# Local attention: one product for values and denominators, and reciprocal norms spread by one bf16 pass over three parts

## What is computed

```python
def l2norm(t):
    return t / jnp.clip(jnp.linalg.norm(t, axis=-1, keepdims=True), 1e-12)
...
h = shift_token(x)
q, k, v = jnp.split(h @ wqkv, 3, axis=-1)            # 8 heads of 64
q = l2norm(q) * qs
k = l2norm(k) * ksc
q, k = rotary_xpos(q, k)
sim = einsum('bhwid,bhwjd->bhwij', bq, bk)           # windows of 64, each sees itself and the one before
attn = jax.nn.softmax(where(mask, -max, sim), axis=-1)
out = jnp.einsum('bhwij,bhwjd->bhwid', attn, bv)
x = x + o @ wo
```

## Time and profile before

| | before |
|---|---|
| median of 3 runs | 6118.09 us (6118.06 to 6119.7) |
| profiled execution, its own time | 6125.03 us |
| its span, first to last instruction | 6123.2 us |
| PE busy | 5316.8 us (87%) |
| DVE busy | 3563.9 us (58%) |
| ACT busy | 3332.0 us (54%) |
| POOL busy | 2568.9 us (42%) |
| mean granted PE clock | 0.946 of 2.4 GHz |

### The profile page before, as it was taken

How to read it: one execution, slowest core, us unless ns; L and a number is a source line. 1 busy time by engine, 2 the same in 40 slices (tenths; PEclk the granted TensorE clock), 3 DMA queues, 4 the chain that set the end, 5 groups by cost and what they waited for, 6 DMA issues and landing times. The chain is left out here.

```text
span 6123.2 us, 113557 instructions
## 1 busy us (share of the span) xinstructions
PE 5316.8 (87%) x39222; PEld 2810.7 (46%) x39222; DVE 3563.9 (58%) x4189; ACT 3332.0 (54%) x4968; POOL 2568.9 (42%) x1902
## 2 busy tenths in 40 slices
PE   5866888888888998999897999899897999787999
PEld 2322555555544554554343554555343444343443
DVE  4757999999964553554354554554554343554444
ACT  4745888888854553554454554455354333443343
POOL 1333999999943662663133662664231000000000
PEclk8986999999999999999898999999899999888999
DMA  1002111111110110110000110111000210001111
GB/s 43 17 10 83 31 31 32 32 30 31 31 52 24 43 43 10 42 42 19 4 15 25 42 42 14 42 41 28 28 15 20 55 41 14 0 0 28 38 33 28
DMA packets 143957, 182.98 MB, mean 30 GB/s; under 512 B 33584, under 2 KB 86960, under 8 KB 142512
## 3 DMA queue, kind: packets, MB, share of 16 engines
q1 hardware_dynamic: 143792, 180.85, 11.1%
HBM read 80.31 MB, written 12.85 MB: 15 GB/s over the span
## 5 line engine op out<-in xcount | busy, mean ns | idle before, releaser
L2502 POOL TENSOR_TENSOR arena<-arena,wbig 128x1024 f32<-128x1024 f32 x512 | 1191.4, 2472 | 107.7 <-ACT arena L2438 107.6
L2489 DVE TENSOR_TENSOR_SCAN arena<-banks,arena 128x1024 f32<-128x1024 f32 x512 | 1140.6, 2278 | 68.4 <-ACT banks L2433 49.4
L963 ACT ACTIVATE arena<-banks,wbig 128x512 f32<-128x512 f32 x512 | 351.8, 687 | 591.2 <-PE banks L921 582.5
L1020 DVE TENSOR_TENSOR arena<-arena 128x512 f32<-128x512 f32 x512 | 353.2, 692 | 470.7 <-ACT arena L963 436.4
L2433 ACT ACTIVATE banks<-banks 128x1020 f32<-128x1020 f32 x512 | 518.1, 1012 | 108.5 <-PE banks L2354 100.9
L1510 POOL TENSOR_TENSOR arena<-arena 128x512 f32<-128x512 f32 x256 | 354.9, 1386 | 527.3 <-DMA arena<-arena 527.3
L635 DVE TENSOR_REDUCE arena<-banks 128x4 f32<-128x1024 f32 (+1 forms) x384 | 401.7, 1046 | 280.0 <-PE banks L462 225.7
L2438 ACT COPY arena<-banks 128x1024 f32<-128x1024 f32 x512 | 520.8, 1017 | 51.2 <-POOL arena L2502 29.9
L571 ACT ACTIVATE Y<-banks 128x2048 f32<-128x2048 f32 x192 | 305.6, 1592 | 306.4 <-PE banks L498 236.4
L931 PE MATMUL banks<-arena,wbig 128*128 128x512 f32 x1024 | 463.5, 598 | 0.0
L921 PE MATMUL banks<-Z,wbig 128*128 x1024 | 459.1, 593 | 0.0
(11 more groups left out here) (304 smaller groups left out, 9887.0 us busy)
## 6 DMA issues: line engine op xcount, KB each, us to landing
arena<-arena SPq DMA_DIRECT2D x1024, 64.0 KB, 2.0
arena<-scratch_g SPq DMA_DIRECT2D x64, 512.0 KB, 10.8
wbig<-wbig SPq DMA_DIRECT2D x48, 240.0 KB, 3.1
wbig<-scratch_d SPq DMA_DIRECT2D x512, 16.0 KB, 1.7
wbig<-scratch_b SPq DMA_DIRECT2D x64, 128.0 KB, 2.2
wbig<-scratch_c SPq DMA_DIRECT2D x64, 128.0 KB, 2.1
arena<-Z SPq DMA_DIRECT2D x64, 128.0 KB, 2.1
wbig<-in_l_ffn SPq DMA_DIRECT2D x1, 4197.0 KB, 12.4
```

The costliest lines, as they stand in the source:

```text
L963: act.activation(hid[e % 2][:, f, :], hbank[f], ACT.Relu, bias=b1[:, e, f:f + 1])\
L1020: last = dve.tensor_tensor(hid[e % 2][:, f, :], hid[e % 2][:, f, :], gate[u][:, e, :], ALU.mult)
L2489: dve.tensor_tensor_scan(own, line(decay_bank[n % 2]), own, 0.0, ALU.mult, ALU.add)\
L2502: pool.tensor_tensor(four(h[par][:, m * 1024:m * 1024 + 1024]), four(us[n % 2]), Bs[par].unsqueeze(1).to_broadcast([128, 4, SEQ]), ALU.mult)\
```

## The change

Three edits in `window_attention_stage`. First, the values tile `v` gets a third slot of ones between the two heads of a group, so that one product with 128 columns of weights gives values in one half of the partitions and denominators in the other; the products with `ones` go away. Head r = 0 has its values in the lower half and its denominators in the upper, head r = 1 the other way round. ACT's logarithm and DVE's multiplication now work on one half of the partitions each, so each becomes two instructions. Second, the reciprocal norm is cut into three bf16 parts: ACT writes it in bf16 (`high`) ahead of the f32 exponential, and DVE makes rest, middle and last part (`norm_parts`), one part to a row within each group of 16. Third, the spreading is a bf16 product over these rows, with a matrix `part_spread` that adds the three parts.

```diff
@@ spread_norms (PE)
                 if n == 0:
-                    pe.wait_ge(act_f.sem, act_f.at(b, "exp"))
+                    pe.wait_ge(dve_p.sem, dve_p.at(b, "parts"))
...
-                    last = pe.matmul(bank[g % 2], k.c64["head_spread"][rows(g), :], rs[rows(g), :],
+                    last = pe.matmul(bank[g % 2], k.cb["part_spread"][rows(g), :], parts[rows(g), :],
@@ values (PE)
                 for c, at, n, first in ((0, 0, 192, 0), (1, 192, 128, 128)):
                     for r in range(2):
-                        pe.matmul(to[half_rows(r), first:first + n], v[par][:, c, 2 * f + r, :],
-                                  prob[f % 2][:, r, at:at + n], start=(c == 0), stop=True, skip_group_check=True)
-                for c, at, n, first in ((0, 0, 192, 0), (1, 192, 128, 128)):
-                    for r in range(2):
-                        last = pe.matmul(to[half_rows(r), SEQ + first:SEQ + first + n], ones[:, 0:WDIM],
-                                         prob[f % 2][:, r, at:at + n], start=False, stop=True, skip_group_check=True)
+                        last = pe.matmul(to[:, r * SEQ + first:r * SEQ + first + n],
+                                         v[par][:, c, f, r:r + 2, :].rearrange("p s d -> p (s d)"),
+                                         prob[f % 2][:, r, at:at + n], start=(c == 0 and r == 0), stop=True,
+                                         skip_group_check=True)
@@ root and reciprocal (ACT)
+                act.activation(high, rs, ACT.Exp, scale=-0.5, bias=k.c64["half_ln"]).then_inc(act_f.sem, 1)
                 act.activation(rs, rs, ACT.Exp, scale=-0.5, bias=k.c64["half_ln"]).then_inc(act_f.sem, 1)
...
-                act.activation(recip[f % 2], obank[f % 2][:, SEQ:2 * SEQ], ACT.Ln).then_inc(act_d.sem, 1)
+                for r in range(2):
+                    last = act.activation(recip[f % 2][half_rows(r), :], obank[f % 2][half_rows(1 - r), r * SEQ:(r + 1) * SEQ],
+                                          ACT.Ln)
+                last.then_inc(act_d.sem, 1)
@@ norm_parts, normalize and trip (DVE)
+            def norm_parts(b):
+                dve.wait_ge(act_f.sem, act_f.at(b, "exp"))
+                dve.scalar_tensor_tensor(out=rs, in0=high, scalar=k.c["rest_minus"], in1=rs, op0=ALU.mult, op1=ALU.add)\
+                    .then_inc(dve_p.sem, 1)
+                dve.wait_ge(dve_p.sem, dve_p.at(b, "rest"))
+                dve.tensor_copy(high, rs).then_inc(dve_p.sem, 1)
+                dve.wait_ge(dve_p.sem, dve_p.at(b, "middle"))
+                dve.wait_ge(pe_f.sem, pe_f.before(b, "norm1"))
+                dve.scalar_tensor_tensor(out=parts, in0=high, scalar=k.c["last_minus"], in1=rs, op0=ALU.mult, op1=ALU.add)\
+                    .then_inc(dve_p.sem, 1)
...
-                dve.tensor_tensor(oT[:, f, :], obank[f % 2][:, 0:SEQ], recip[f % 2], ALU.mult).then_inc(dve_n.sem, 1)
+                for r in range(2):
+                    last = dve.tensor_tensor(oT[half_rows(r), f, :], obank[f % 2][half_rows(r), r * SEQ:(r + 1) * SEQ],
+                                             recip[f % 2][half_rows(r), :], ALU.mult)
+                last.then_inc(dve_n.sem, 1)
...
                 reduce(b, 3)
+                if more:
+                    norm_parts(b + 1)
                 normalize(b, 1)
```

More of the change, by code:

```diff
@@ L1085, in window_attention_stage @@
     pe_w = Steps(k, "mixed", ["wo"], BATCH)
-    act_f = Steps(k, "squares", ["cp0", "sq0", "sq1", "cp2", "sq2", "sq3", "ln", "exp", "hb"], BATCH)
+    act_f = Steps(k, "squares", ["cp0", "sq0", "sq1", "cp2", "sq2", "sq3", "ln", "high", "exp", "hb"], BATCH)
     act_e = Steps(k, "exponentials", ["e0", "v", "e1", "e2", "e3"], BATCH)
@@ L1095, in window_attention_stage @@
     pool_f = Steps(k, "sides", [f"{s}{f}" for f in groups for s in ("sin", "add")] + [f"low{f}" for f in groups], BATCH)
+    dve_p = Steps(k, "norm_parts", ["rest", "middle", "parts"], BATCH)
     pool_h = Steps(k, "shifted", ["low", "high"], BATCH)
@@ L1109, in window_attention_stage @@
     rs = take(TILE)
+    high, parts = k.arena.take_bf16(TILE), k.arena.take_bf16(TILE)
     cos_w, sin_w = take(TILE), take(TILE)
@@ L1112, in window_attention_stage @@
     qkb = pairs(k.arena.take_bf16(8 * SEQ), 8)
-    v = [take(2 * 512).rearrange("p (c h d) -> p c h d", c=2, h=WHEADS) for _ in range(2)]
+    v = [take(2 * 4 * 192).rearrange("p (c f s d) -> p c f s d", c=2, f=4, s=3) for _ in range(2)]
     prob = [pairs(take(2 * 320), 2) for _ in range(2)]
@@ L1122, in window_attention_stage @@
     obank = [k.psum[:, 6 + n, :] for n in range(2)]
-    cleared = Count(k, "cleared", 5)
+    cleared = Count(k, "cleared", 7)
     ones = k.c["ones"]
@@ L1135, in _ @@
             dve.memset(mx, 0.0).then_inc(cleared.sem, 1)
+            for par in range(2):
+                dve.memset(v[par][:, :, :, 1, :], 1.0).then_inc(cleared.sem, 1)
             for m, (scale, partner) in enumerate(((w["qs"], w["qp"]), (w["ks"], w["kp"]))):
@@ L1141, in _ @@
                     .then_inc(cleared.sem, 1)
-            dve.wait_ge(cleared.sem, cleared.at(5))
+            dve.wait_ge(cleared.sem, cleared.at(7))
     with nc.Block() as block:
@@ L1348, in values_in @@
                 for c in range(2):
-                    last = act.copy(v[par][:, c, :, :].rearrange("p h d -> p (h d)"), bank[c])
+                    last = act.copy(v[par][:, c, :, 0:3:2, :], bank[c].rearrange("p (f r d) -> p f r d", f=4, r=2))
                 last.then_inc(act_e.sem, 1)
@@ L1411, in _ @@
         def _(dve):
-            for s in (dve_f, dve_r, dve_n, dve_y):
+            for s in (dve_f, dve_r, dve_n, dve_y, dve_p):
                 s.prime(dve)
@@ L1491, in _ @@
             cosine(0, 3)
+            norm_parts(0)
             for g in groups:
@@ L2754, in constants @@
         "reverse": np.tile(np.arange(8, 0, -1, dtype=f), (128, 1)),
+        "rest_minus": -((feature[:, None] % 16 == 1) | (feature[:, None] % 16 == 2)).astype(f),
+        "last_minus": -(feature[:, None] % 16 == 2).astype(f),
         "eps5": np.full((128, 1), 1e-5, f),
@@ L2768, in constants @@
     later = token[None, :] > token[:, None]
-    b = {"ident": eye, "ones": np.ones((128, 128), f), "causal_qk": np.where(later, NEG, 0), "causal_kq": np.where(later.T, NEG, 0)}
+    part_spread = ((feature[:, None] % 32 // 16 == feature[None, :] // 64) & (feature[:, None] % 16 < 3)).astype(f)
+    b = {"part_spread": part_spread, "ident": eye, "ones": np.ones((128, 128), f), "causal_qk": np.where(later, NEG, 0), "causal_kq": np.where(later.T, NEG, 0)}
     b = {name: bf16_pairs(a) for name, a in b.items()}
```

## The result

The changed kernel takes 6474.18 us (median of 4, 6468.39 to 6481.51) against 6118.9 us (6118.06 to 6122.79): a ratio of 1.058, interval 1.0567 to 1.0593. That is 5.8% slower where 5.4% was forecast.

The account below looks back on a forecast made before the run. PE was taken to bound the kernel. A trip's 3.8 us longer path plus 1.56 us slower clock, 5.3 us over 60 trips, gave 320 us; with 12 us once-a-layer costs, the median forecast was 6450 us, range 6260 to 6540.

Parts of the forecast that it names:

- The wait moves to DVE's last part: PE's first spreading in each trip waits for `norm_parts`, starting 5.86 us later; PE idles 6.3 us in place of 0.4.
- POOL in the way of the parts: DVE's three part operations, 1.92 us alone, lose 2.60 us more a trip to POOL working on SBUF.
- the third rival: Each part waits for a whole POOL operation, clock low for two pieces a trip: 6616 us; chance 0.12, whole or half.
- the mean block of the first: Each of DVE's three part operations loses only the mean 0.42 us to POOL, 1.26 together: 6370 us; chance 0.18.
- ACT's additions hidden: ACT's second logarithms, 0.38 us each, and extra exponential, 0.72 us, end before DVE is ready, so cost nothing.
- The path from spreading to `maxima`: On PE, from first spreading to `maxima(b + 1, 0)`: 3.74 us in place of 5.83, a gain of 2.09.
- The clock: PE's idle time lowers the granted clock for spreading, scores and values behind it: 1.56 us a trip.
- The second rival: PE's clock stays at 2.4 GHz: 94 us less, 6356, or 6276 with fewer POOL waits; chance 0.17 together.
- Joint product saves nothing: On PE, the replaced half-array products already ran side by side; 0.04 us a call saved, counted as nothing.
- The sum: Path 3.8 plus clock 1.56 make 5.3 us a trip; 60 trips give 320, plus 12: median 6450 us.
- Once a layer: Memsets, one more logarithm and half `normalize` at the end, and the first batch: 12 us over four layers.
- The fourth rival: Parts are ready when `values(b, 1)` ends, PE's work decides and saves 1.2 us a trip: 6046 us; chance 0.04.

Follow-up runs that it names:

- the parts from the bank: Changed kernel with the clipped sum, logarithm, exponential and rest kept in a PSUM bank instead of an SBUF tile: 6359.11 us, 1.0396.
- the tightened one: Kernel before with bf16 parts and spreading, parts and cosines read from PSUM banks, root and parts earlier: 6031.16 us; with the joint product 6116.88 us.
- filler: Changed kernel with six f32 products, results thrown away, on PE in the idle time before the first spreading: 6321.85 us, 1.0326.
- cosines from the bank: Kernel before with cosines reading the projection in its PSUM bank, not the SBUF copy, all four ahead of `clip`: 6092.27 us; with the joint product 6137.07 us.
- the parts alone: Kernel before with the three parts and bf16 spreading, keeping the old values, `reciprocal` and `normalize`: 6445.08 us, 1.0532.

## Why the prediction was right, and where its sizes were off

- **The wait moves to DVE's last part.** Right, and the main term. The spreading waited for L1449 381.1/64 = 5.95 us each time, 5.78 in the trips without the first batches; 6.3 was forecast. From `maxima` to the next first spreading the mean grew from 19.36 to 24.59 us, 5.2 where 5.86 was charged.
- **POOL in the way of the parts.** The mechanism was right, shown by the parts from the bank. Its size was too large: 2.60 us charged, 3.76 − 1.92 = 1.84 measured in the means. Two of the three wait for POOL in a trip, not all three: the cast and the last in most, the first and the cast in ten. Neither the full block of the third rival nor the mean block of the first (1.26) fits; the rule of the Trainium skill taken to its bound, 3.8, was further off.
- **The cosines in front of them.** Not foreseen. The 0.34 us of `normalize` were charged at 0.34. In the trip shown, and in most of the first layer, the pair went from 2.45 us to 3.47; in the other layers it is a little shorter than before. Over all trips the pair's mean grew only from 2.51 to 2.64 us, so the term was small in the total.
- **ACT's additions hidden.** Right for the exponential: it ended 1.75 us before DVE took it up. The second logarithm was called free as well. It was not priced where it stands between PE and `normalize(b, 1)`. In the changed kernel 5.95 us of idle time hid that; in the tightened one it did not.
- **The path from spreading to `maxima`.** 3.74 us forecast at full clock; with filler the mean was 3.85.
- **The clock.** This is the mis-sized term: 1.56 us charged, 2.3 to 2.5 measured by the filler. The 1.56 came from a stretch with a mean granted clock of 0.63; here it was 0.55 in the trip shown and 0.51 in the mean, over the whole path. For the four stretches about 0.9 was forecast, and it is 0.83 to 0.86. So spreading to `maxima` took 6.15 us where 5.30 was forecast. The second rival (no slowing) is refuted.
- **Joint product saves nothing.** Nearly right on PE. At full clock, from its start to that of a product right behind it, a group takes 1.15 us in the median (1.14 was forecast); the pair of products that it replaces took 1.24, not 1.18, so 0.09 us a group are saved. Its price in this change, 29 us, is the sum of what was charged for its second halves (0.34 a trip, 9 of once-a-layer terms), but that is luck: settled trips don't show the 0.34, and half of the 29 lies in the first layer. The same edit cost 62 us alone, 45 with cosines from the bank and 86 in the tightened kernel.
- **The sum.** The two errors nearly cancel: 5.2 in place of 5.86, and 6.15 in place of 5.30. The mean trip grew by 5.20 us, from 25.52 to 30.72, where 5.33 was forecast; 60 trips make 312 us in place of 320. (The paths and trips of the forecast are those of one settled trip, 5.83 and 25.11 us; the means are 6.14 and 25.52.)
- **Once a layer.** Too small, and hidden in the total: 12 us charged, 44 measured beside the 312, in the profiled executions. From PE's last product before a layer to its first spreading it takes 24.5 us in the mean where it took 17.2, 29 us in the four layers. The first batch was charged at most 1 us, but its three parts stand ahead of the first spreading and all wait for POOL (1.74, 1.37 and 1.63 us), and with the parts alone 24 of these 29 us are there. The ends of the layers add 8, and some 7 lie elsewhere. So the closeness of 6474 to 6450 is partly luck: one term too large, two too small.
- **The fourth rival**, a gain once the parts come early enough: its mechanism exists. It took the parts out of SBUF, DVE's queue in another order, the cosines out of POOL's way, and no joint product: 6031.16 us. That this lies near the 6046 that was worked out is luck: the bf16 spreading brought 46 us where 72 were counted, and the other 42 came from edits that the rival didn't have.

## What to carry to other kernels

A product that is faster on the engine that bounds the kernel is paid for by whoever prepares its input: add up the chain from the last thing that engine gave to the first that it needs back, with every handover, before counting its columns. Where two engines work out of the same memory side by side, put one operand of the operation on the critical path in the other memory; that alone gave 115 us here. And price an added microsecond by what stands behind it: the joint product cost 29, 45, 62 and 86 us in four surroundings, each known to within 11 to 20 us.

## What was not expected of the hardware

- Six useless products a trip made the kernel 152 us faster, since PE then kept a granted clock of 0.94 and more in place of 0.86.
- In a trip of the first layer, a delay of 0.34 us on DVE was followed by a pair of cosines that took 1.04 us more, since POOL now started its operation 0.01 us ahead of them. In most trips of the other layers the same delay cost the pair nothing. The cast's 1.37 us in all 64 executions, with min and max 4 ns apart, reads as DVE and POOL alternating in a fixed phase rather than meeting at random; no run varied that phase by itself.
- An operation on 64 partitions takes as long as one on 128: `normalize` 0.86 us for two on 64 and 0.42 for one on 128, both 256 columns wide.
